# Expert rows that carry their place and weight, in a one-core decoder layer

## The chip, the core and the metric

The kernel runs on one core of a Trainium2 chip. The metric is the device time of one launch in microseconds (us). Five engines work side by side: PE (TensorE) with its weight loads (PEld), DVE (VectorE), ACT (ScalarE), POOL (GpSimd) and SP (SyncE, which here issues plain DMAs). They meet only through semaphores and barriers.

## What is computed

Four sequences of 512 tokens with 256 features go through a Mamba block, a self- and cross-attention block and this feed-forward block; the change lies in the last one:

```python
abel_out = gelu(xn @ abel_w + abel_b)
logits = xn @ moe_gate_w + moe_gate_b
topw, topi = top_k(logits, 2); topw = softmax(topw)
w_dense = sum(one_hot(topi, 8) * topw[..., None], axis=-2)
h = gelu(einsum('bsd,edh->ebsh', xn, ew1) + eb1)
eo = einsum('ebsh,ehd->ebsd', h, ew2) + eb2
moe_out = einsum('ebsd,bse->bsd', eo, w_dense)
for i in range(3): moe_out = moe_out @ expm(gens[i])
gate = sigmoid(concatenate([abel_out, moe_out]) @ gc_w + gc_b)
return residual + abel_out * (1 - gate) + moe_out * gate
```

There are 8 experts with 512 hidden features, and each of the 2048 tokens goes to 2 of them: 4096 rows in all.

## The kernel before

The program is a row of blocks with barriers between them. Block b = 0 to 4 (`for b in range(NB + 1)`) begins sequence b (projections, convolution, time steps) and ends sequence b-1 (output projection, residual, norms, the abel branch, routing). Between them lie the scan and the attention of sequence b, which the change leaves alone. I call blocks 1 to 3 the middle blocks and b = 4, which only ends, the last block.

**Routing** (end of a block, `choose`, `place`, `weigh`). DVE picks two experts a token. TensorE counts how many tokens of each expert stand ahead (`rank_mm`). `place` (L726) turns this into row numbers in `rows_in`, a DRAM tensor with a region of 2048 rows for each expert, and writes them to `route`; `weigh` (L742) then works out the two weights of each token. When the row numbers are there (`route_ready`), POOL scatters the normalised rows `xn2` in 8 indirect DMAs of 128 rows (L503), then adds the abel branch to the residual x1 (L508). SP stores what is kept for later: `kept_sel`, `kept_abel`, `kept_res`, `kept_route` (L465).

**Expert part** (from L1406). 23 tiles of 256 rows, each of one expert: every expert's rows in whole tiles, then spare ones. DVE works out from the counts which expert and which rows a tile has (L1592 to L1620, the tables) and which bias (L1632 to L1638). SP reads both numbers from the table (`value_load`, L1415 and L1422) and issues the tile's rows (L1427, 256 KB) and weights (L1416 and L1418, 512 KB each; three weight buffers). For a tile PE turns the rows (`rows_up`, L1485), multiplies into the hidden layer (`hidden`, 16 matmul instructions), ACT applies gelu (L1569), PE multiplies into the output (`output`, 16 instructions), DVE copies it to `eo` (L1666) and SP stores that to `rows_out` (L1432). DVE's `rows_down` (L1627) takes the turned rows from PSUM with the norm's scale and shift. PE's order is hidden(i+1), rows_up(i+2), output(i). SP's order for tile i is

```python
rows_load(i + 3)
weights(i + 2)      # waits for the output matmuls of tile i - 1
rows_store(i)       # waits for DVE's copy of tile i
```

and every second tile from 4 on SP brings back a sequence's `kept_abel` and `kept_res` (L1451, L1453).

**Last part.** 16 steps q of 128 tokens. POOL gathers the two expert rows of each token from `rows_out` (L1472, 32 indirect DMAs, buffers for 8 steps) at places that DVE works out in `places`. PE makes the bias part (`biased`, the weights of the token on the experts' `eb2`), DVE adds the two rows times their weights (L1675, L1678), PE turns the sum (L1536), ACT copies it (L1582), PE multiplies it by the rotation `Wrot` (`rotated`). DVE takes the gate's product over the row (L1683) and the difference to the abel branch (L1686); per sequence follow the gate (L1691, L1692, ACT L1575) and the result rows (L1701), which SP stores (L1457). All matmuls there and in the expert part are recorded at L165, transpositions at L1485 and L1536.

## Time and profile before

| | us |
|---|---|
| median of 3 runs (2150.28 to 2151.87) | 2150.67 |
| the profiled execution, its own time | 2149.31 |
| its span in the trace | 2147.6 |
| PE busy | 1607.7 (75%) |
| PEld busy | 768.3 (36%) |
| DVE busy | 1416.9 (66%) |
| ACT busy | 827.5 (39%) |
| POOL busy | 640.9 (30%) |
| mean granted clock of TensorE | 0.866 |

"Granted clock" is the share of TensorE's full speed (1.00 is 2.4 GHz, 0.50 is 1.2 GHz). In rows of the timeline the first number is the start, the second how long a group of instructions took from first start to last end; in brackets stands the idle time of the engine ahead of it and what ended that. A row SPq or POOLq is a DMA issue or a wait on that queue. "remote" is a releaser that the profile doesn't know.

### The profile page before, as it was taken

Reading aid. Unit: us, or ns where it says so; the run is one execution under the profiler, and the core shown is the slowest. Engines: PE = TensorE matmul, PEld = TensorE weight load, DVE = VectorE, ACT = ScalarE, POOL = GpSimd, SP = SyncE. Lnnn points to the kernel's source line nnn. Section 1 sums busy time; section 2 is a strip of 40 time slices with the busy share of each in tenths; the row PEclk is TensorE's granted clock in tenths of the full one; section 3 lists DMA queues with packets and bytes.
Section 4 is the critical chain, followed back from the end, with each engine's and each line's share of the span. In section 5 each row is a group of like instructions: output and inputs, shape, how many; then the busy total and the mean of one; then the engine's idle time right before and its main releaser. Section 6 shows DMA issues by size and latency. Waiting matters only on the chain. (4 is left out here: it accounts for less than half of the span.)

```text
span 2147.6 us, 19868 instructions
## 1 busy us (share of the span) xinstructions
PE 1607.7 (75%) x6786; PEld 768.3 (36%) x6786; DVE 1416.9 (66%) x2091; ACT 827.5 (39%) x1552; POOL 640.9 (30%) x396
## 2 busy tenths in 40 slices
PE   4887699774977898739867997646679984488976
PEld 2454223242543222315432332212322222467753
DVE  6996878277987775659968873779687835221225
ACT  4542166543422566244422664433115661111210
POOL 2763311206655021136532112076340112100041
PEclk9899699986997899959987998789879996799975
DMA  5821720021006220030035200210062100466631
GB/s 178 289 70 47 157 38 1 1 79 45 1 0 167 38 38 1 0 123 1 0 95 109 38 2 0 82 37 0 5 156 41 21 1 9 153 200 196 198 98 61
DMA packets 125101, 149.27 MB, mean 70 GB/s; under 512 B 16000, under 2 KB 107784, under 8 KB 122952
## 3 DMA queue, kind: packets, MB, share of 16 engines
q1 hardware_dynamic: 121928, 139.61, 23.9%
q0 software_dynamic: 3072, 8.39, 1.2%
q8 instruction: 54, 0.88, 0.2%
q14 instruction: 47, 0.39, 0.1%
HBM read 96.47 MB, written 51.09 MB: 69 GB/s over the span
## 5 line engine op out<-in xcount | busy, mean ns | idle before, releaser
L165 PE MATMUL PS<-arena 128*32 128x512 f32 (+11 forms) x4126 | 883.4, 454 | 122.2 <-DMA arena<-in_ew 25.4
L165 PEld LDWEIGHTS PS<-arena 128*32 128x32 f32 (+3 forms) x4126 | 367.1, 128 | 615.8 <-ACT arena L1338 276.5
L1338 ACT ACTIVATE arena<-PS 128x512 f32<-128x512 f32 (+3 forms) x768 | 375.4, 541 | 378.3 <-PE PS L165 377.1
L968 POOL TENSOR_TENSOR arena<-arena 128x1024 f32<-128x1024 f32 x128 | 302.1, 2362 | 186.5 <-DVE arena L992 147.0
L1358 DVE TENSOR_REDUCE maxs<-PS 128x1 f32<-128x1024 f32 x256 | 302.3, 1217 | 78.4 <-PE PS L165 78.3
L992 DVE TENSOR_TENSOR_SCAN arena<-PS,arena 128x1024 f32<-128x1024 f32 x128 | 292.1, 2282 | 9.3 <-POOL arena L968 9.3
L948 ACT ACTIVATE PS<-arena,A_neg 128x511 f32<-128x511 f32 x256 | 166.0, 681 | 261.3 <-DVE arena L992 193.1
L165 PE MATMUL PS<-arena,ident 128*128 128x512 f32 (+1 forms) x560 | 259.8, 590 | 5.4 <-DVE arena L1001 5.4
L1191 POOL TENSOR_TENSOR arena<-xn 128x512 f32<-128x512 f32 x16 | 20.3, 1267 | 585.4 <-ACT xn L1326 585.4
L165 PE MATMUL PS<-bc,bc_sel 96*128 96x512 bf16 x128 | 52.3, 408 | 149.2 <-DVE arena L1001 98.1
L1001 DVE TENSOR_TENSOR arena<-arena,PS 128x1024 f32<-128x1024 f32 x128 | 156.3, 1221 | 7.1 <-PE PS L165 3.0
L1385 DVE RECIPROCAL arena<-arena 128x512 f32<-128x512 f32 x16 | 53.6, 3348 | 142.5 <-POOL arena L1191 142.5
L165 PEld LDWEIGHTS PS<-arena,ident 128*128 128x128 f32 x560 | 109.5, 199 | 91.7 <-issue 74.5
L1362 DVE TENSOR_REDUCE maxs<-PS 128x1 f32<-128x512 f32 (+3 forms) x256 | 106.9, 477 | 19.9 <-PE PS L165 18.8
L1569 ACT ACTIVATE arena<-PS,arena 128x256 f32<-128x256 f32 x92 | 38.6, 471 | 196.2 <-PE PS L165 196.2
L1472 POOL DMA_INDIRECT arena<-rows_out,arena x32 | 30.6, 957 | 239.3 <-DMA rows_out<-arena 224.5
L1627 DVE TENSOR_SCALAR arena<-PS,gam,bet 128x256 f32<-128x256 f32 x46 | 22.9, 539 | 108.3 <-PE PS L1485 108.3
L165 PEld LDWEIGHTS PS<-bc,bc_sel 96*128 96x128 bf16 x128 | 12.5, 98 | 202.6 <-DVE arena L1001 147.2
L503 POOL DMA_INDIRECT rows_in<-arena,route x32 | 34.8, 1089 | 162.4 <-DVE route L739 153.9
L1125 DVE TENSOR_TENSOR arena<-arena 128x512 f32<-128x512 f32 x40 | 50.0, 1249 | 32.9 <-ACT arena L1080 32.9
L1096 POOL TENSOR_TENSOR arena<-arena 128x512 bf16<-128x512 f32 x40 | 46.3, 1157 | 66.9 <-DVE arena L1126 66.9
L165 PE MATMUL PS<-wp,arena 128*128 128x256 f32 x128 | 37.2, 462 | 34.3 <-PEq L172 34.3
(251 smaller groups left out, 1807.8 us busy)
## 6 DMA issues: line engine op xcount, KB each, us to landing
arena<-in_ew SPq DMA_DIRECT2D x46, 512.0 KB, 5.2
arena<-stack_parts SPq DMA_DIRECT2D x288, 64.0 KB, 3.7
rows_in<-nil SPq DMA_DIRECT2D x17, 1024.0 KB, 11.2
arena<-b_rows SPq DMA_DIRECT2D x16, 1024.0 KB, 7.7
stack_parts<-arena SPq DMA_DIRECT2D x40, 384.0 KB, 3.1
arena<-stack_parts SPq DMA_DIRECT2D x96, 128.0 KB, 4.6
arena<-rows_in SPq DMA_DIRECT2D x23, 256.0 KB, 2.9
rows_out<-arena SPq DMA_DIRECT2D x23, 256.0 KB, 2.1
```

Source lines behind the costliest of these rows:

```text
L165: return nc.tensor.matmul(o, l, r, start=start, stop=stop)
L948: last = nc.scalar.activation(decay(i)[:, k, 1:T], delta[:, 2 * kh + k, 1:T], ACT.Exp, scale=A_neg[:, 2 * kh + k, n:n + 1])
L968: nc.gpsimd.tensor_tensor(b_sb[i % 2], u[:, 2 * kh:2 * kh + 2, :], Brow[:, n, :].unsqueeze(1).to_broadcast([P, 2, T]), ALU.mult).then_inc( ...
L992: nc.vector.tensor_tensor_scan(h_sb[i % 2].rearrange(flat), decay(i).rearrange(flat), b_sb[i % 2].rearrange(flat), 0.0, ALU.mult, ALU.add)\
L1001: nc.vector.tensor_tensor(g_sb[i % 2], h_sb[i % 2], bank(6).unsqueeze(1).to_broadcast([P, 2, T]), ALU.mult).then_inc(S["g_done"], 1)
L1096: nc.gpsimd.tensor_tensor(pt[i % NPT][:, 2, :], r_sb[i % 2], pt[i % NPT][:, 1, :], ALU.subtract)\
L1125: link(nc.vector.tensor_tensor(r_sb[i % 2], f_sb[i % 2], pt[i % NPT][:, 0, :], ALU.subtract))
L1338: nc.scalar.activation(probs[(HG * s + h) % NPR][:, 0:N], bank(4 + n % 2)[:, 0:N], ACT.Exp, scale=HD ** -0.5).then_inc(S["ring_read"], 1)
L1358: last = nc.vector.reduce_max(maxs[:, g % 2, r, h:h + 1], PS[:, 2 * s:2 * s + 2, :].rearrange("p a n -> p (a n)"), AXX)
L1362: last = nc.vector.reduce_max(maxs[:, g % 2, q, HG + h:HG + h + 1], bank(2 * s + c_)[:, 0:(q + 1) * P], AXX)
L1385: nc.vector.reciprocal(R2, R1).then_inc(S["norm_ready"], 1)
L1569: nc.scalar.activation(hid[i % 2][:, m, :], o, ACT.Gelu, bias=eb1_of[:, i, m:m + 1])\
```

## The change

A row in `rows_in` grows from 256 to 272 numbers: the 256 features, at 256 the number of the place where its result belongs (first or second choice, times 2048, plus the token), at 257 the token's weight, then zeros. For this POOL writes places and a second copy of the rows into `xn2`, and DVE's `weigh` now runs ahead of `place`, since the weight goes out with the row. Rows that no token fills carry the place 4096, which the scatter leaves out.

Of the 23 tiles the first eight are fixed: tile e is the first 256 rows of expert e. The tables are only worked out for the other 15. The weights of the first three tiles are loaded in the last block, into memory that it doesn't use.

In the expert part DVE copies each row's place and weight out of the loaded rows (`noted`), scales the output by the weight as it takes it from PSUM, and POOL scatters it straight to its place in `picked_rows` (two indirect DMAs a tile, 46 in all). SP no longer stores results, and asks for weights i+3 as soon as the output matmuls of tile i are done; the kept tensors come behind them, one every second tile.

In the last part SP reads plain pieces of `picked_rows`. DVE adds the two rows with one operation. The bias part is multiplied through the rotation once, ahead of the tiles (`eb2R`), and joins the rotation's accumulation; the gate's product is a 257th column of the rotation (`turn`), so DVE's product over the row is gone, and `kept_route` with it.

```diff
-NTILE = (TOPK * NB * T + NE * (RT - 1)) // RT
-SPARE = NTILE - TOPK * NB * T // RT
-ROWS = NE * CAP + SPARE * RT
+NEXTRA = (TOPK * NB * T - 1) // RT
+NTILE = NE + NEXTRA
+ROWS = NE * CAP + RT
+RW = 272
+AT_ID, AT_W = DM, DM + 1
+NOWHERE = TOPK * NB * T
...
-    rows_in = nc.dram_tensor("rows_in", (ROWS, DM), F32).ap()
-    rows_out = nc.dram_tensor("rows_out", (NTILE * RT, DM), F32).ap()
+    rows_in = nc.dram_tensor("rows_in", (ROWS, RW), F32).ap()
+    picked_rows = nc.dram_tensor("picked_rows", (NOWHERE, DM), F32).ap()
...
+                    if not begins:
+                        for i in range(NWB):
+                            weights_load(sp, i, i)
...
-                        sp.wait_ge(S["route_ready"], TT + 2)
-                        keep(kept_route[b - 1], route[:].rearrange("p f t -> p (f t)"))
                         if not begins:
-                            sp.wait_ge(S["kept"], 4 * 16)
+                            sp.wait_ge(S["kept"], 3 * 16)
...
+                        nc.gpsimd.memset(xn2[:, :, :, AT_W + 1:RW], 0.0).then_inc(S["rows_told"], 1)
+                        for j in range(TOPK):
+                            nc.gpsimd.iota(xn2[:, j, :, AT_ID], pattern=[[P, TT]], base=(j * NB + b - 1) * T,
+                                           channel_multiplier=1, allow_small_or_imprecise_dtypes=True)\
+                                .then_inc(S["rows_told"], 1)
+                        nc.gpsimd.tensor_copy(xn2[:, 1, :, 0:DM], xn2[:, 0, :, 0:DM]).then_inc(S["rows_told"], 1)
+                        pool.wait_ge(S["rows_told"], 4)
+                        pool.wait_ge(S["weighed"], 2)
                         pool.wait_ge(S["route_ready"], 1)
                         for t in range(TT):
                             for j in range(TOPK):
                                 nc.gpsimd.indirect_dma_start(
                                     rows_in, bass.IndirectOffsetOnAxis(ap=route[:, j, t:t + 1].bitcast(I32), axis=0),
-                                    xn2[:, t, :], None).then_inc(rows_stored, 16)
+                                    xn2[:, j, t, :], None).then_inc(rows_stored, 16)
...
                 def weights(i):
-                    if i >= NWB:
-                        sp.wait_ge(S["eo_mm"], i - NWB + 1)
-                    e = sp.value_load(where[0:1, 0, i:i + 1].bitcast(I32), min_val=0, max_val=NE - 1)
-                    sp.dma_start(ew1[i % NWB], w["ew1"][bass.ds(e, 1), :, :].rearrange("a (k p) n -> p (a k) n", p=P))\
-                        .then_inc(weights_in[i % NWB], 16)
-                    sp.dma_start(ew2[i % NWB], w["ew2"][bass.ds(e, 1), :, :].rearrange("a (k p) n -> p (a k) n", p=P))\
-                        .then_inc(weights_in[i % NWB], 16)
-
+                    sp.wait_ge(S["eo_mm"], i - NWB + 1)
+                    if i < NE:
+                        e = i
+                    else:
+                        if i == NE:
+                            sp.wait_ge(S["tables"], 1)
+                        e = sp.value_load(where[0:1, 0, i - NE:i - NE + 1].bitcast(I32), min_val=0, max_val=NE - 1)
+                    weights_load(sp, i, e)
 
                 def rows_load(i):
                     if i >= NXB:
-                        sp.wait_ge(S["rows_mm"], i - NXB + 1)
-                    sp.dma_start(rows[i % NXB], rows_in[bass.ds(row(i), RT), :].rearrange("(r p) n -> p r n", p=P))\
+                        sp.wait_ge(S["rowsT_ready"], KM * (i - NXB + 1))
+                    if i < NE:
+                        r = i * CAP
+                    else:
+                        if i == NE:
+                            sp.wait_ge(S["tables"], 1)
+                        r = sp.value_load(where[0:1, 1, i - NE:i - NE + 1].bitcast(I32), min_val=0, max_val=ROWS - RT)
+                    sp.dma_start(rows[i % NXB], rows_in[bass.ds(r, RT), :].rearrange("(r p) n -> p r n", p=P))\
                         .then_inc(rows_back[i % NXB], 16)
 
-                def rows_store(i):
-                    sp.wait_ge(S["eo_ready"], i + 1)
-                    sp.dma_start(rows_out[i * RT:(i + 1) * RT, :].rearrange("(r p) n -> p r n", p=P), eo[i % 3])\
-                        .then_inc(eo_stored[i % 3], 16)
-
-                sp.wait_ge(S["tables"], 1)
-                rows_load(0)
-                weights(0)
-                rows_load(1)
-                weights(1)
-                rows_load(2)
-                back(route_all.rearrange("p b f t -> p b (f t)"), kept_route.rearrange("b p f -> p b f"))
-                back(sel_all.rearrange("e (b t) -> e b t", b=NB), kept_sel.rearrange("b e t -> e b t"))
+                def pick(q):
+                    if q >= NPK:
+                        sp.wait_ge(S["summed"], q - NPK + 1)
+                    src = picked_rows.rearrange("(j q p) n -> q p j n", j=TOPK, p=P)
+                    sp.dma_start(picked[q % NPK], src[q]).then_inc(picked_in[q % NPK], 16)
+
+                sp.wait_ge(rows_stored, 16 * TOPK * TT * NB)
+                for i in range(3):
+                    rows_load(i)
+                sp.dma_start(sel_all.rearrange("e (b t) -> e b t", b=NB), kept_sel.rearrange("b e t -> e b t"))\
+                    .then_inc(S["sel_back"], 16)
                 for i in range(NTILE):
                     if i + 3 < NTILE:
                         rows_load(i + 3)
-                    if i + 2 < NTILE:
-                        weights(i + 2)
-                    rows_store(i)
-                    if i >= 4 and i % 2 == 0 and i < 4 + 2 * NB:
-                        b = i // 2 - 2
-                        sp.dma_start(ab_all[:, TT * b:TT * (b + 1), :], kept_abel[b].rearrange("(t p) n -> p t n", p=P))\
-                            .then_inc(S["rest_back"], 16)
-                        sp.dma_start(res_all[:, TT * b:TT * (b + 1), :], kept_res[b].rearrange("(t p) n -> p t n", p=P))\
-                            .then_inc(S["rest_back"], 16)
+                        weights(i + 3)
+                    if i % 2 == 0 and i < 4 * NB:
+                        b, part = i // 4, i % 4
+                        if part == 0:
+                            sp.dma_start(ab_all[:, TT * b:TT * (b + 1), 0:DM],
+                                         kept_abel[b].rearrange("(t p) n -> p t n", p=P)).then_inc(S["rest_back"], 16)
+                        else:
+                            sp.dma_start(res_all[:, TT * b:TT * (b + 1), :],
+                                         kept_res[b].rearrange("(t p) n -> p t n", p=P)).then_inc(S["rest_back"], 16)
+                for i in range(NEB):
+                    sp.wait_ge(eo_stored[i], 16 * RS * len(range(i, NTILE, NEB)))
+                for q in range(NQ):
+                    pick(q)
...
-                pool.wait_ge(S["moved"], 1)
-                for i in range(3):
-                    pool.wait_ge(eo_stored[i], 16 * len(range(i, NTILE, 3)))
-                for q in range(NQ):
-                    if q >= NGB:
-                        pool.wait_ge(S["summed"], q - NGB + 1)
-                    for j in range(TOPK):
+                for i in range(NTILE):
+                    pool.wait_ge(S["noted"], 2 * (i + 1))
+                    pool.wait_ge(S["eo_ready"], RS * (i + 1))
+                    for r in range(RS):
                         nc.gpsimd.indirect_dma_start(
-                            picked[j][q % NGB], None, rows_out,
-                            bass.IndirectOffsetOnAxis(ap=slot[:, q // TT, j, q % TT:q % TT + 1].bitcast(I32),
-                                                      axis=0)).then_inc(picked_in[q % NGB], 16)
+                            picked_rows,
+                            bass.IndirectOffsetOnAxis(ap=row_id[i % NIB][:, r:r + 1].bitcast(I32), axis=0),
...
                     last.then_inc(S["moeT_mm"], 1)
 
                 def rotated(q):
-                    pe.wait_ge(S["moeT_ready"], q + 1)
                     if q >= 4:
                         pe.wait_ge(S["diffed"], q - 3)
+                    o = bank(4 + q % 4)[:, 0:DM + 1]
+                    mm(o, sel_all[:, q * P:(q + 1) * P], eb2R, True, False)
+                    pe.wait_ge(S["moeT_ready"], q + 1)
                     for k in range(KM):
-                        last = mm(bank(4 + q % 4)[:, 0:DM], moeT[q % 2][:, k, :], Wrot[:, k, :], k == 0, k == KM - 1)
+                        last = mm(o, moeT[q % 2][:, k, :], turn[:, k, :], False, k == KM - 1)
                     last.then_inc(S["rot_mm"], 1)
 
...
+                    nc.vector.tensor_copy(row_id[i % NIB].bitcast(I32), rows[i % NXB][:, :, AT_ID]).then_inc(S["noted"], 1)
+                    nc.vector.tensor_copy(row_w[i % NIB], rows[i % NXB][:, :, AT_W]).then_inc(S["noted"], 1)
...
+                dve.wait_ge(rows_stored, 16 * TOPK * TT * NB)
+                nc.vector.tensor_copy(turn[:, :, 0:DM], Wrot[:]).then_inc(S["turn_ready"], 1)
+                for k in range(KM):
+                    nc.vector.tensor_tensor_reduce(out=dots2, in0=Wrot[:, k, :], in1=gcw[:, DM:2 * DM], scale=1.0,
+                                                   scalar=0.0, op0=ALU.mult, op1=ALU.add,
+                                                   accum_out=turn[:, k, DM:DM + 1]).then_inc(S["turn_ready"], 1)
+                    dve.wait_ge(S["turn_ready"], 2 + k)
                 rows_down(0)
+                extra_tiles()
                 rows_down(1)
...
+                    dve.wait_ge(S["noted"], 2 * (i + 1))
+                    if i >= NEB:
+                        dve.wait_ge(eo_stored[i % NEB], 16 * RS * (i // NEB))
+                    for r in range(RS):
+                        nc.vector.tensor_scalar(eo[i % NEB][:, r, :], bank(6 + i % 2)[:, r * DM:(r + 1) * DM],
+                                                row_w[i % NIB][:, r:r + 1], None, ALU.mult).then_inc(S["eo_ready"], 1)
 
                 def summed(q):
-                    dve.wait_ge(picked_in[q % NGB], 32 * (q // NGB + 1))
-                    dve.wait_ge(S["eb_mm"], q + 1)
+                    dve.wait_ge(picked_in[q % NPK], 16 * (q // NPK + 1))
                     if q >= NAB:
                         dve.wait_ge(S["moeT_mm"], q - NAB + 1)
-                    b, t = q // TT, q % TT
-                    link(nc.vector.scalar_tensor_tensor(acc[q % NAB], picked[0][q % NGB],
-                                                        route_all[:, b, TOPK, t:t + 1],
-                                                        bank(q % 2)[:, 0:DM], ALU.mult, ALU.add))
-                    nc.vector.scalar_tensor_tensor(acc[q % NAB], picked[1][q % NGB], route_all[:, b, TOPK + 1, t:t + 1],
-                                                   acc[q % NAB], ALU.mult, ALU.add).then_inc(S["summed"], 1)
-
-                def gated(q):
+                    nc.vector.tensor_tensor(acc[q % NAB], picked[q % NPK][:, 0, :], picked[q % NPK][:, 1, :], ALU.add)\
+                        .then_inc(S["summed"], 1)
+
+                def differ(q):
                     dve.wait_ge(S["rot_mm"], q + 1)
-                    link(nc.vector.tensor_tensor_reduce(out=dots2, in0=bank(4 + q % 4)[:, 0:DM],
-                                                        in1=gcw[:, DM:2 * DM], scale=1.0, scalar=0.0,
-                                                        op0=ALU.mult, op1=ALU.add, accum_out=gates[:, 0, q:q + 1]))
-                    nc.vector.tensor_tensor(ab_all[:, q, :], bank(4 + q % 4)[:, 0:DM], ab_all[:, q, :], ALU.subtract)\
-                        .then_inc(S["diffed"], 1)
+                    nc.vector.tensor_tensor(ab_all[:, q, :], bank(4 + q % 4)[:, 0:DM + 1], ab_all[:, q, :],
+                                            ALU.subtract).then_inc(S["diffed"], 1)
 
```

SP in the expert part, between the weights of one tile and those of the next. Before:

```order
L1415 TENSOR_LOAD arena [waits eo_mm]
L1415 ISA x2
L1416 ISA
L1416 DMA arena<-in_ew 128x2x512
L1418 DMA arena<-in_ew 128x4x256
L1432 DMA rows_out<-arena 128x2x256 [waits eo_ready]
L1422 TENSOR_LOAD arena [waits rows_mm]
L1422 ISA x2
L1427 ISA
L1427 DMA arena<-rows_in 128x2x256
```

With the change:

```order
L1432 TENSOR_LOAD arena [waits eo_mm]
L1432 ISA x2
L465 ISA
L465 DMA arena<-in_ew 128x2x512
L467 DMA arena<-in_ew 128x4x256
L1443 TENSOR_LOAD arena [waits rowsT_ready]
L1443 ISA x2
L1444 ISA
L1444 DMA arena<-rows_in 128x2x272
```

The store, and with it the wait for DVE's copy (`eo_ready`), is gone from SP's queue, and the rows wait for DVE's `rows_down` instead of for PE.

DVE at the end of a middle block, around the row numbers. Before (`fchain` is the chain of these small operations):

```order
L734 TENSOR_TENSOR s_pos<-PS,base 128x32 [waits rank_mm,fchain]
L737 TENSOR_TENSOR s_nth<-s_gt,s_pos 128x32 [waits fchain]
L738 TENSOR_REDUCE row_f<-s_nth 128x4 [waits fchain]
L737 TENSOR_TENSOR s_nth<-s_eq,s_pos 128x32 [waits fchain]
L738 TENSOR_REDUCE row_f<-s_nth 128x4 [waits fchain]
L739 CAST route<-row_f 128x8 [waits fchain]
L740 TENSOR_TENSOR base<-base,PS 128x8
L744 TENSOR_SCALAR s_den<-sel_e 128x4 [waits sel_e,fchain]
```

With the change:

```order
L754 TENSOR_SCALAR s_den<-sel_e 128x4 [waits sel_e,fchain]
L755 RECIPROCAL s_den<-s_den 128x4 [waits fchain]
L756 TENSOR_TENSOR sel<-sel,sel_ex 128x32 [waits fchain]
L757 TENSOR_TENSOR sel<-sel,s_den 128x32 [waits fchain]
L760 TENSOR_TENSOR s_nth<-s_gt,sel 128x32 [waits sel_ready]
L761 TENSOR_REDUCE arena<-s_nth 128x4 [waits fchain]
L760 TENSOR_TENSOR s_nth<-s_eq,sel 128x32 [waits weighed]
L761 TENSOR_REDUCE arena<-s_nth 128x4 [waits fchain]
L767 TENSOR_TENSOR s_pos<-PS,base 128x32 [waits rank_mm,weighed]
```

Eight operations of the weighing stand ahead of the placing now; the CAST to `route`, for which POOL waits, comes after them.

PE in the last part, one step. Before:

```order
L1536 MATMUL PS<-ident,arena 128x128 [waits moeT_ready,summed]
L1536 MATMUL PS<-ident,arena 128x128
L165 MATMUL PS<-eb,arena 128x256 [waits summed]
L165 MATMUL PS<-Wrot,arena 128x256 [waits diffed,moeT_ready]
L165 MATMUL PS<-Wrot,arena 128x256
```

With the change:

```order
L1555 MATMUL PS<-ident,arena 128x128 [waits moeT_ready,summed]
L1555 MATMUL PS<-ident,arena 128x128
L168 MATMUL PS<-arena 128x257 [waits diffed]
L168 MATMUL PS<-arena 128x257 [waits moeT_ready]
L168 MATMUL PS<-arena 128x257
```

The number of matmuls stays, with one column more each; the bias matmul is now the first of the rotation's accumulation.

## Rows read from the trace of the kernel before

**Rows 1.** stretches: us, busy (instructions) of PE, PEld, DVE, ACT, POOL, PEclk, DMA, GB/s
```profile
1853.80:2060.00 206.20, 179.94 (x821) 152.10 (x820) 42.66 (x93) 40.12 (x94) 0.00 (x0) 0.96 0.59 184
2060.00:2147.60 87.60, 55.43 (x128) 32.54 (x128) 37.09 (x113) 6.63 (x20) 30.62 (x32) 0.53 0.25 75
```

**Rows 2.** chain of waits, expert part: start us, us, what
```profile
1866.57 0.70 DVE arena L1666
...
1868.87 0.28 SPq L1415
...
1870.07 5.14 DMA arena<-in_ew
1875.25 3.72 PE PS L165 x16
1878.97 0.44 PE PS L1485 x4
1879.41 3.47 PE PS L165 x16
...
1967.08 6.90 DMA arena<-in_ew
...
2045.47 13.83 PE PS L165 x64
2059.32 0.70 DVE arena L1666
```

**Rows 3.** waits of SP's queue, expert part to the end: us, times, longest
```profile
SPq L1432 <- DVE arena L1666: 133.1, 23, 12.7
```

**Rows 4.** timeline, end of the first middle block: start us, us, what
```profile
491.78 0.17 DVE L744 TENSOR_SCALAR s_den<-sel_e 128x4 f32<-128x4 f32 x1
...
493.32 0.19 DVE L751 TENSOR_REDUCE route<-s_nth 128x4 f32<-128x32 f32 x1
...
506.18 0.50 SPq L465 DMA_DIRECT2D kept_route<-route  x1
```

**Rows 5.** timeline, convolution in the first middle block, beside POOL
```profile
445.39 2.58 POOL L498 TENSOR_TENSOR x<-x,arena 128x1024 f32<-128x1024 f32 x1 [16.49 <-DVE arena L663]
...
445.80 4.29 DVE L690 SCALAR_TENSOR_TENSOR arena<-arena,conv_w 128x512 f32<-128x512 f32 x3
...
450.59 2.33 DVE L690 SCALAR_TENSOR_TENSOR arena<-arena,conv_w 128x512 f32<-128x512 f32 x3
```

**Rows 6.** timeline, from the barrier to the first tile
```profile
1838.47 0.07 DVE L1592 MEMSET arena<- 128x8 f32 x1 [13.46 <-PEq L461]
...
1844.42 0.41 SPq L1427 DMA_DIRECT2D arena<-rows_in  x1
...
1847.14 0.72 PEld L1485 LDWEIGHTS PS<-ident,arena 128*128 128x128 f32 x4 [25.09 <-DMA arena<-rows_in]
...
1853.76 1.06 PE L165 MATMUL PS<-arena 128*128 128x256 f32 x2
```

**Rows 7.** timeline, last part, DVE, PE and ACT
```profile
2068.32 0.69 PE L1536 MATMUL PS<-ident,arena 128*128 128x128 f32 x2 [7.13 <-DVE arena L1678]
...
2088.14 0.39 ACT L1582 ACTIVATE arena<-PS 128x256 f32<-128x256 f32 x1 [9.07 <-remote]
...
2104.95 0.82 ACT L1582 ACTIVATE arena<-PS 128x256 f32<-128x256 f32 x2 [16.42 <-remote]
...
2115.12 0.63 PE L1536 MATMUL PS<-ident,arena 128*128 128x128 f32 x2
...
2118.70 0.63 PE L1536 MATMUL PS<-ident,arena 128*128 128x128 f32 x2
...
2142.57 1.67 DVE L1701 SCALAR_TENSOR_TENSOR arena<-arena 128x256 f32<-128x256 f32 x4
```

**Rows 8.** two short stretches of the last part, columns as in rows 1
```profile
2115.00:2120.00 5.00, 5.00 (x13) 2.86 (x11) 2.98 (x10) 0.77 (x2) 0.00 (x0) 0.50 0.00 0
2076.00:2080.00 4.00, 4.00 (x10) 2.40 (x10) 2.42 (x9) 0.38 (x1) 3.08 (x4) 0.50 0.37 106
```

279 lines of the change are left out of this document (133 added, 146 removed).

## The prediction

> **What bounds the kernel now.** I read the busy time by stretches first, then the chain of waits, then the timeline at the joints. The expert part takes 206.2 us and the last part 87.6 us [rows 1]; the rest of the span, 1853.8 us, is the attention and scan part, which the change touches only at four places. In the expert part TensorE is busy 179.9 of 206.2 us at a mean granted clock of 0.96, the DMA engines 0.59: neither is full. The chain shows why. One turn covers two tiles: the result copy on DVE (1866.57), SP's store and address work, a flight of the next weights (5.14), then 3.72 + 0.44 + 3.47 of matmuls to the next copy [rows 2]. The weights of tile i+3 can be asked for only when SP has come past the store of tile i, and SP sat 133.1 us in those 23 waits [rows 3]. So the turn is weight latency plus one tile of TensorE work, and not two tiles of work.
>
> The last part is TensorE at half clock: the granted clock is 0.53 [rows 1], one step of 16 starts every 3.58 us (2115.12 to 2118.70) [rows 7], and inside 2115 to 2120 TensorE is busy 5.00 of 5.00 us at 0.50 [rows 8]. There are holes on top: ACT sat idle 9.07 and 16.42 us before two copies whose inputs had long been made [rows 7], released by nothing the profile can name. They lie where POOL issues one gather after another, 3.08 us of 4 [rows 8].
>
> **The sum, part by part** (against the profiled span, 2147.6 us).
>
> 1. *Three middle blocks.* The weighing now stands ahead of the placing, so the row numbers come later by what those eight DVE operations take: 491.78 to 493.51, 1.73 us [rows 4]. POOL's eight scatters wait for these numbers, and the barrier waits for what follows them. The store of the routing table, 0.50 us on SP ahead of the barrier [rows 4], goes. POOL also gets a small memset, two iotas and a copy of 1024 elements a partition. They end long before POOL needs the routing, but beside a POOL operation of that size DVE's three convolution steps took 4.29 us where they take 2.33 [rows 5], and the copy falls on the same steps. The copy's own time is not in the trace: bounds are 0 (it misses them) and 1.96 us (the whole difference); I take 1.2, nearer the row, as the copy reads one input and that addition two. Per block +1.73 - 0.50 + 1.2 = 2.4, three times +7.3 us. The Trainium skill (SBUF — State Buffer, "Who interferes with whom") says that a DVE instruction with two SBUF inputs waits out a GpSimd instruction that reads SBUF, whole. By that rule each block would pay up to the copy's full length. The 4.29 us agree with it.
>
> 2. *Into the first tile.* The last such block pays 1.73 us and about 0.5 of the copy (its DVE work there reads PSUM), so the barrier moves from 1838.47 to 1840.7 [rows 6]. Behind it stood the tables and the first weights: rows issued at 1844.42, their transposes at 1847.14, the first expert matmul at 1853.76 [rows 6]. Now the first eight tiles have fixed places, three tiles of weights are loaded during the last block, and the rows go out at once: issue 0.41 and flight 2.3 (1844.83 to 1847.14) give 1843.4. TensorE first makes the turned bias: about 1.7 us of DVE work, then four instructions at 0.53 (two took 1.06 [rows 6]), to 1844.5; transposes and the copies down about 2.4 more. First matmul at 1846.9: -6.8 us. Bounds: -9 without the bias work in the way, -4 if the copies go slowly.
>
> 3. *First tiles.* Tile 1's rows now come up behind the first hidden layer, so its hidden layer waits for a copy down: a transposition and two copies at low clock, 2.5 us. The new tables (some 25 small DVE operations) lie beside the first hidden layer. +2.5 us.
>
> 4. *Steady tiles.* SP no longer stores; it waits for the output matmuls of tile i and asks for weights i+3 at once. From the read of the expert's number to the landing a turn takes 6.34 us (1868.87 to 1875.21) [rows 2]; add 0.9 for scatters in the same queue engines (a gather pair moves 106 GB/s at a share of 0.37 [rows 8], so 256 KB are about 0.9 us of all engines). 7.2 us stand against 3.46 + 0.44 + 3.47 = 7.4 us of TensorE work on tiles that are already there (64 matmuls took 13.83, so 16 take 3.46 [rows 2]). The weights just fit. From the first result (1866.57) to the last output matmul (2059.32) were 192.8 us [rows 2]. The work in it is 43 groups of 16 and 20 transpositions: 43 x 3.46 + 20 x 0.44 = 157.6. As the fit is tight I add 8 us of small waits (0.4 a tile; bounds 0 and 20, the latter if each second tile waits 2 us). -27.2 us. DVE has two copies and two scaled results a tile and POOL two scatters: both under half of 7.4 us, with three result buffers. The kept tensors are now behind the weights in SP's queue, where today they are ahead of them: the flight of 6.90 us [rows 2] should go.
>
> 5. *Joint.* Today from the last output matmul to the first transposition of the last part 9.0 us pass (2059.32 to 2068.32) [rows 2, 7]: copy, store, gather. Now: two scaled copies, two scatters, their landing, a plain read. About 9.6, +0.6 us.
>
> 6. *Last part.* Plain reads replace 32 gathers; the gate's product rides as column 257 of the rotation; the bias matmul moves into the rotation's accumulation. TensorE keeps its instructions: 16 x 3.58 = 57.3 us if the clock stays. After the last rotation DVE has one difference, a clamp, ACT's exponential, two small operations and 1.67 us of results [rows 7]: about 3.3 us, 60.6 in all. Today 75.9 (2068.32 to 2144.24) [rows 7]. -15.3 us: some 13 from the holes, which end with the burst of gathers, 2 from shorter DVE work behind the last rotation.
>
> Sum: +7.3 - 6.8 + 2.5 - 27.2 + 0.6 - 15.3 = -38.9 us, a span of 2108.7. The profiled execution took 2149.31 us, 1.7 more than its span, and the median of the runs is 1.4 above it: 2108.7 + 3.1 = **2112 us**.
>
> **Rivals.**
>
> *The clock rises in the last part* (0.20). For: without the bias matmul in between, today's last steps run on at 2136 us and the clock comes up right behind them; the continuous expert part is at 0.96 [rows 1]. Against: 5.00 of 5.00 busy at 0.50 [rows 8], for over 20 us, with the same instructions that the change keeps. At 2.4 GHz a step is six instructions at 0.216, transpositions and the same gaps, about 2.1 us; 16 x 1.5 = 23 us less: 2089. The Trainium skill (TensorE: Matmul & The Clock Gate, "Part 1: The HAM clock gate") says that the throttled state is the default and activity releases it. By that rule the time is 2089; the 0.50 at full busy time speaks against it here.
>
> *The holes come with indirect DMAs wherever they are* (0.10). The last part lost 13 us over 32; 46 are now spread over the expert part. For: nothing in the trace names their cause. Against: the 32 scatters of the blocks show none. +13 us: 2125.
>
> *Weights still pace the tiles* (0.08). With the scatters in the way the flight becomes 6.90 + 0.9, the latency 9.0, and a tile costs (9.0 + 7.36)/2 = 8.2 instead of 7.16 + 0.36. 22 x 0.68 = +15: 2127.
>
> *Slower than before* (0.03). The same loop, with scattered rows of 1 KB and weights fighting for the DMA engines: each weight load then lands late and TensorE idles, falling to half clock between tiles. The whole gain is gone when the stretch of point 4 costs 38.9 us more than forecast, (165.6 + 38.9)/22 = 9.3 us a tile, so a latency of 11.2 us, a flight near 10 where 5.14 and at most 6.90 are seen [rows 2]. At a flight of 11 the time is 2112 + 38.9 + 11 = 2162.
>
> **How the numbers follow.** The forecast has 0.59, with its own range 2102 to 2123 from the bounds of points 1, 2 and 4. The range 2086 to 2128 takes in the clock case and the two cases above 2120. A measurement of this kernel tells 0.2% (4 us) from no change. Faster by more: all but the last rival and its edge, 0.95; within 0.02; slower 0.03.
>
> **What would show it.** Right: SP waits for TensorE's output matmuls, not for DVE's copy; a tile starts each 7.2 to 7.8 us; the first expert matmul stands some 7 us nearer to the barrier and more; steps of 3.6 us in the last part with no unnamed idle time; blocks one to three 2 to 3 us longer each. Wrong: TensorE waiting for weights in most tiles, a granted clock of 1.0 in the last part, or unnamed idle time in the expert part.

## The result

| | before | changed |
|---|---|---|
| median of 4 runs each | 2150.53 us | 2097.24 us |
| lowest to highest | 2150.28 to 2151.87 | 2095.23 to 2100.65 |
| span of the profiled execution | 2147.6 us | 2093.5 us |

The ratio is 0.9753, with a 95% interval from 0.9736 to 0.977: 53 us less, where 38.9 were forecast. The time lies in the range given, 15 us below the forecast. The kernel before is not always at 2150: beside four of the experiments (weights asked for first, the margin, the first idle gathers, the filling matmuls), which ran on another chip than the later ones, it took 2133 us, beside all others 2149 to 2151. I call these four the first group. The changed kernel itself was not timed beside the 2133; with added work that nothing waits for it took 2097.93 us there. The experiments show where most of these 17 us lie.

Busy time by stretches of the changed kernel: from the first expert matmul to the last result, and the last part. The columns are those of [rows 1].

```profile
1848.78:2020.10 171.32, 169.26 (x824) 148.15 (x824) 52.95 (x180) 40.13 (x94) 42.92 (x44) 1.00 0.64 203
...
2028.69:2086.90 58.21, 58.17 (x128) 33.38 (x128) 17.79 (x52) 6.43 (x19) 0.00 (x0) 0.50 0.27 88
```

In the expert part TensorE went from 179.9 of 206.2 us [rows 1] to 169.3 of 171.3, at full clock throughout. In the last part it is busy 58.17 of 58.21 us at 0.50.

The chain of waits through the steady tiles, which answers to [rows 2] (start us, us, what):

```profile
1854.88 3.69 PE PS L168 x16
1858.57 0.44 PE PS L1503 x4
1859.01 6.91 PE PS L168 x32
1865.92 0.44 PE PS L1503 x4
1866.35 6.91 PE PS L168 x32
```

There is no transfer and no copy on it any more: a tile costs 7.35 us (6.91 + 0.44), and this goes on to 2020.02. SP's waits in the whole kernel at the two lines that ask for weights (L1432 is the address read in `weights`, L465 the load itself), and TensorE's from 1850 to 2020 (engine, line, waited for: us in total, times, longest):

```profile
SPq L1432 <- PE PS L168: 63.3, 15, 4.6
SPq L465 <- PE PS L168: 34.0, 4, 16.9
```

```profile
PE PS L168 <- DVE arena L1624: 2.0, 1, 2.0
```

SP now waits for TensorE and not for DVE's copy [rows 3]. TensorE's only wait there is the 2.0 us before its second hidden layer.

The timeline at the four places of the other changes:

```profile
457.51 2.98 DVE L711 SCALAR_TENSOR_TENSOR arena<-arena,conv_w 128x512 f32<-128x512 f32 x3
...
457.73 1.43 POOL L518 COPY arena<-arena 128x1024 f32<-128x1024 f32 x1
...
493.98 0.17 DVE L772 CAST route<-row_f 128x8 int32<-128x8 f32 x1
...
505.20 2.35 POOL L529 TENSOR_TENSOR x<-x,arena 128x1024 f32<-128x1024 f32 x1
...
508.56 4.65 POOL L984 TENSOR_TENSOR arena<-arena 128x1024 f32<-128x1024 f32 x2 [1.02 <-POOLq L473]
...
1843.08 1.40 SPq L1444 DMA_DIRECT2D arena<-rows_in  x3
...
1846.28 1.12 PE L1503 MATMUL PS<-ident,arena 128*128 128x128 f32 x4
...
1848.78 3.69 PE L168 MATMUL PS<-arena 128*128 128x256 f32 x16 [1.39 <-DVE arena L1624]
...
1862.50 0.88 DVE L1683 TENSOR_SCALAR arena<-PS,arena 128x256 f32<-128x256 f32 x2 [2.32 <-PE PS L168]
...
2020.05 0.87 DVE L1683 TENSOR_SCALAR arena<-PS,arena 128x256 f32<-128x256 f32 x2 [2.58 <-PE PS L168]
...
2028.69 1.28 PE L1555 MATMUL PS<-ident,arena 128*128 128x128 f32 x4 [8.68 <-DVE arena L1690]
...
2032.92 0.63 PE L1555 MATMUL PS<-ident,arena 128*128 128x128 f32 x2
...
2036.51 0.63 PE L1555 MATMUL PS<-ident,arena 128*128 128x128 f32 x2
...
2088.22 1.68 DVE L1709 SCALAR_TENSOR_TENSOR arena<-arena 128x256 f32<-128x256 f32 x4
```

Read against the same points of before ([rows 2], [rows 6], [rows 7]), the 54.1 us between the spans divide as follows. The third column is the prediction's term, cut at the same points (the 2.2 us of point 2 for the barrier stand in the first row).

| stretch | measured | forecast |
|---|---|---|
| to the barrier: 1838.47 to 1843.07 | +4.6 | +9.5 |
| barrier to first expert matmul: 15.3 to 5.7 | -9.6 | -9.1 |
| first expert matmul to first result: 12.8 to 13.7 | +0.9 | +2.5 |
| first to last result: 192.8 to 157.6 | -35.2 | -27.2 |
| last result to first step of the last part: 9.0 to 8.6 | -0.4 | +0.6 |
| first step to the last output on DVE: 75.9 to 61.2 | -14.7 | -15.3 |
| behind it: 3.4 to 3.6 | +0.2 | 0 |

The row of the first result depends on the clock: in this execution it was at 1.00 from the first hidden layer on. In a second execution of the changed kernel (under "The holes of the last part") the same stretch took 16.0 us and not 13.7, since the clock was still at the lower level when the first hidden layer began (columns as above):

```profile
1851.10:1855.00 3.90, 3.84 (x9) 3.15 (x10) 3.27 (x18) 0.05 (x1) 0.00 (x0) 0.50 0.04 10
```

### The profile page after: what moved, and what is told of

Its sections match the earlier page's. It is cut to its first block and busy times, and to the rows that moved or that the text cites. A ratio compares the mean times of both kernels' runs of the same rounds, so it can differ in the third digit from the quotient of the medians.

```text
span 2093.5 us, 19873 instructions
## 1 busy us (share of the span) xinstructions
PE 1611.3 (77%) x6792; PEld 767.3 (37%) x6792; DVE 1406.0 (67%) x2088; ACT 828.1 (40%) x1554; POOL 660.2 (32%) x427
## 5 line engine op out<-in xcount | busy, mean ns | idle before, releaser
L168 PE MATMUL PS<-arena 128*128 128x256 f32 (+9 forms) x4226 | 929.0, 458 | 97.2 <-ACT arena L1354 23.4
L168 PEld LDWEIGHTS PS<-arena 128*32 128x32 f32 (+4 forms) x4226 | 389.9, 131 | 607.5 <-ACT arena L1354 276.9
L1489 POOL DMA_INDIRECT picked_rows<-arena x46 | 45.4, 986 | 135.4 <-DVE arena L1683 114.8
L168 PE MATMUL PS<-xT,in_w 128*128 128x512 f32 x128 | 58.5, 616 | 3.4 <-DVE xT L813 3.4
L1595 ACT ACTIVATE arena<-PS,arena 128x256 f32<-128x256 f32 x60 | 25.2, 471 | 85.2 <-PE PS L168 85.2
```

The lines of the kernel that those rows point to most:

```text
L168: return nc.tensor.matmul(o, l, r, start=start, stop=stop)
L1489: nc.gpsimd.indirect_dma_start(picked_rows, bass.IndirectOffsetOnAxis(ap=row_id[i % NIB][:, r:r + 1].bitcast(I32), axis=0), eo[i % NEB][:, ...
```

## The experiments

The ratio given with each run is that of its median to that of the kernel before, measured beside it on the same chip, with its 95% interval. The texts in quotes are the expectations, as they stood before each run.

### Weights asked for first

In the kernel before, in SP's queue:

```diff
                 weights(1)
                 rows_load(2)
+                weights(2)
...
-                    if i + 2 < NTILE:
-                        weights(i + 2)
+                        weights(i + 3)
                     rows_store(i)
```

> The kernel before, with one edit in the expert part's SP queue: the weights of tile i+3 are asked for as soon as the output matmuls of tile i are done, ahead of the store of tile i; nothing else. Theory (the order of the queue is the whole gain of the steady tiles): from the end of the output matmuls to the landing about 0.5 + 0.5 + 5.1 = 6.1 to 6.7 us, against 7.36 us of TensorE work that is there; the waits go, the stretch from the first result to the last output matmul falls from 192.8 to 158 to 162 us, the time to 2116 to 2122 us. Rival (the stores and their traffic matter too): every second tile still waits 1 to 2 us, the stretch stays above 172 us, the time above 2130.

Measured: 2104.17 us, ratio 0.9857 [0.9841, 0.9873]; the kernel before took 2133.13 beside it. The waits of TensorE in the expert part, of the kernel before:

```profile
PE PS L165 <- DMA arena<-in_ew: 25.4, 13, 5.7
```

and of this one:

```profile
PE PS L165 <- DMA arena<-in_ew: 0.7, 1, 0.7
```

From the first to the last result 161.0 us pass (1870.74 to 2031.69) where it was 192.8. So 31.8 of the 35.2 us come from one thing, when SP asks; a second execution on another chip gave 160.8. The time came out lower than both theories said because the last part, with its 32 gathers in place, took 61.0 us and had no unnamed idle time at all. This is as long as the last part of the changed kernel (61.2). The new one saves some 3 us of DVE work behind the last rotation, but the old one has two shorter steps at its end (2.13 us from 2091.07 to 2093.20), which make no bias matmul and in which the clock rises. The missing holes spoke against the cause that the prediction names for the holes and led to the next three groups.

### The margin of the fit

In the changed kernel, on SP:

```diff
                     sp.wait_ge(S["eo_mm"], i - NWB + 1)
+                    sp.wait_ge(S["eo_ready"], RS * (i - NWB + 1))
```

> The changed kernel; SP asks for the weights of tile i+3 only when DVE has also scaled and copied the result of tile i (about 0.9 us later). Measures the margin of the fit. Theory (the flight is still near 5.1 us beside the scatters, so some 1.0 us of margin): 0 to +3 us on 2097. Rival (the fit is bare, the flight longer beside scatters): each steady tile waits 0.5 to 0.9 us, +10 to +18 us.

Measured: 2105.3 us, ratio 0.9867 [0.9848, 0.9885]. First to last result takes 164.9 us, 7.4 more, of which the waits show 4.6:

```profile
PE PS L168 <- DMA arena<-in_ew: 4.6, 8, 2.3
```

The other 2.6 us stand in TensorE's own busy time (160.11 us against 157.51). The time lies between what both theories give (8 us more than 2097): a delay of 0.9 us makes TensorE wait for weights eight times. The margin is real but under a microsecond for a third of the tiles. "The weights just fit" was right; the allowance of 8 us for it was too large. It was not for nothing, either: of eight executions in which this stretch of the changed kernel was left as it is, three took 157.6 to 157.7 us, four 158.2 to 159.6 and one 161.0, that one with three waits for weights, 2.7 us together.

### The holes of the last part

First with gathers added to the changed kernel, whose data nobody reads; POOL issues them behind its last scatters:

```diff
+                for q in range(NQ):
+                    g, had = ghost_in[q % 4]
+                    if q >= 4:
+                        pool.wait_ge(g, had + 32 * (q // 4))
+                    if q >= 8:
+                        pool.wait_ge(S["summed"], q - 7)
+                    for j in range(TOPK):
+                        nc.gpsimd.indirect_dma_start(
+                            ghost[2 * (q % 8) + j], None, rows_in,
+                            bass.IndirectOffsetOnAxis(ap=route[:, j, q % TT:q % TT + 1].bitcast(I32),
+                                                      axis=0)).then_inc(g, 16)
```

> The changed kernel; beside its last part POOL issues the 32 indirect gathers that the kernel before had there, one row of 1088 bytes a partition, into buffers that nobody reads; nothing waits for them. Theory (the unnamed holes of the part come with the burst of indirect DMAs): ACT and DVE stand still again for some 10 to 16 us, the last part takes 71 to 77 instead of 61 us, the time 2107 to 2113. Rival (the holes were the gathers' own late data, which the profile failed to name): 0 to +3 us.

Measured: 2097.93 us, no unnamed idle time. This looked like a refutation, but the kernel before took 2133.13 beside it, 17 less than at first. So both kernels ran again, unchanged:

> The kernel before, unchanged. In the run with the weights asked for first, the burst of 32 gathers was there and ran without one unnamed idle time, last part 61.0 us; with 32 idle gathers added to the changed kernel likewise. Theory (the holes of the profiled run are no property of the kernel but of that run): the last part takes about 63 us from the first transposition to the last output instead of 75.9, no idle time without a name, span 2131 to 2136. Rival (they belong to this kernel's own burst, which starts at another moment than in the other two): the holes are there again at the same steps, span near 2147.

> The changed kernel, unchanged, beside the others of this call. Both theories: 2095 to 2099, no unnamed idle time; it gives the ratio against the kernel before in the same hour, 0.982 to 0.984 if the holes were of that run alone, 0.975 if not.

Measured: the kernel before 2150.74 (the other runs of it beside the experiments of this group 2149.22), the changed one 2098.61, ratio 0.9763 [0.9744, 0.9783]. The holes of the kernel before are back at the same steps, of the same length as in [rows 7]:

```profile
2089.05 0.38 ACT L1582 ACTIVATE arena<-PS 128x256 f32<-128x256 f32 x1 [10.06 <-remote]
...
2105.16 0.82 ACT L1582 ACTIVATE arena<-PS 128x256 f32<-128x256 f32 x2 [15.74 <-remote]
```

The theory as it was written fell: the holes are no accident of one execution. What was left was a condition that holds for a whole group of runs and only shows with some kernels. Two kernels of the first group were run again, on a third chip, to tell whether it is the gathers:

> The kernel before with the weights asked for first, a second time, since the kernel before ran in 2133 us beside its first run and in 2149 beside the later ones. Theory (the holes are a state of the hour, whatever the kernel that has the gathers): if the kernel before takes 2149 in this call too, the holes are in this run's last part as well, 74 to 76 us instead of 61.0, the time 2117 to 2120. Rival (they depend on where the burst falls): no holes, 2104, whatever the kernel before takes. If the kernel before takes 2133 in this call, it tells nothing new on this.

> The changed kernel with 32 idle gathers beside its last part, a second time, for the same reason. Theory (in the hours in which the kernel before takes 2149, a burst of indirect gathers brings the holes): 10 to 16 us of unnamed idle time, 2107 to 2113. Rival (the holes need gathers whose data DVE waits for, or this burst is not enough): 2098.

Measured, with the kernel before at 2149.28: weights first 2115.93 us, ratio 0.9841 [0.9826, 0.9857], 12 more than in the first group, its last part 75.6 us in place of 61.0. Idle gathers 2118.55 us, ratio 0.9854 [0.9839, 0.9869], 20 more than the changed kernel. The timeline of the latter:

```profile
2029.65 0.99 POOL L1507 DMA_INDIRECT arena<-rows_in,route  x1 [1.92 <-issue]
...
2047.43 0.38 ACT L1624 ACTIVATE arena<-PS 128x256 f32<-128x256 f32 x1 [6.30 <-remote]
...
2059.36 0.43 DVE L1712 TENSOR_TENSOR arena<-PS,arena 128x257 f32<-128x257 f32 x1 [14.04 <-remote]
...
2064.95 0.38 ACT L1624 ACTIVATE arena<-PS 128x256 f32<-128x256 f32 x1 [17.14 <-remote]
...
2068.62 0.95 POOL L1507 DMA_INDIRECT arena<-rows_in,route  x1 [0.30 <-issue]
...
2074.78 0.42 DVE L1712 TENSOR_TENSOR arena<-PS,arena 128x257 f32<-128x257 f32 x1 [14.39 <-remote]
```

ACT and DVE are idle for up to 17 us although their inputs are there for most of that time (ACT's copy at 2064.95 had its two transpositions at 2050.84); POOL issues one gather each 1.25 us all the while, and some 5 us behind its last one the stand-still ends. Nothing waits for these gathers, so it is not their data. Last, the same 32 gathers, each pair behind the sum of its step:

```diff
-                    if q >= 8:
-                        pool.wait_ge(S["summed"], q - 7)
+                    pool.wait_ge(S["summed"], q + 1)
```

> The changed kernel with the same 32 idle gathers beside its last part, now one pair to a step of TensorE (each pair waits for the sum of its step, so POOL issues for 2.5 of each 3.6 us and not without a break). In the run before, the first stand-still came 14.6 us after the first of the unbroken burst (17.8 us in the kernel before) and the last ended with it. Theory (it is the unbroken burst): no unnamed idle time, 2097 to 2100. Rival (the number or the mean rate of the gathers is what counts): holes from some 15 us in, 2108 or more. If the kernel before takes 2133 in this call, it tells nothing.

Measured: 2099.7 us, ratio 0.9768 [0.9751, 0.9784], the kernel before at 2151.13. No idle time without a name is left. The gathers did not come in pairs, though, as the expectation has it. DVE's sums run ahead of the steps, so POOL found most pairs released already: 16 in a row (19.8 us), a pause of 7.0 us, eight, a pause of 4.5 us, eight:

```profile
2029.29 0.99 POOL L1506 DMA_INDIRECT arena<-rows_in,route  x1 [5.31 <-DVE arena L1706]
...
2048.11 0.95 POOL L1506 DMA_INDIRECT arena<-rows_in,route  x1 [0.30 <-issue]
2056.08 0.94 POOL L1506 DMA_INDIRECT arena<-rows_in,route  x1 [7.02 <-DVE arena L1706]
...
2070.57 0.94 POOL L1506 DMA_INDIRECT arena<-rows_in,route  x1 [4.54 <-DVE arena L1706]
...
2079.32 0.95 POOL L1506 DMA_INDIRECT arena<-rows_in,route  x1 [0.30 <-issue]
```

So the gathers bring the holes, but not their data and not their number alone: two pauses took all of them away. With 30 or 32 in a row the first stand-still began 15 to 19 us behind the first gather, after 12 to 16 of them; the longest row here is 16. That fits a limit on the unbroken run. Whether it is that or the mean rate over the whole (32 in 51 us in place of 40) no run tells apart. The bursts of eight in the blocks (10.1 us) and the 46 scatters of the expert part, two a tile, show none. Open too is what the engines wait for, and why 32 in a row cost nothing in the first group: it ran at another time and on another chip than the later groups, and the two can't be told apart.

### The clock of the last part

In the changed kernel, on TensorE, ahead of the last part, 20 matmuls whose result nobody reads:

```diff
+                for _ in range(20):
+                    mm(bank(0)[:, 0:RT], rowsT[0][:, 0, 0:P], rowsT[1][:, 0, :], True, True)
                 pe.wait_ge(S["eo_ready"], RS * NTILE)
```

> The changed kernel; TensorE makes 20 matmuls of 128x256 (40 instructions, 8.6 us at full clock) into an unused bank between the last output matmul and the first transposition of the last part. Theory (the pause of 8.6 us is what lets the clock fall, and the last part would hold it): the granted clock is 1.0 in the last part, a step 1.8 us in place of 3.60, the last part 33 instead of 61 us, the time near 2069. Rival A (the last part's steps cannot hold the clock): it starts at 1.0 and falls back within it, gain in between, 2075 to 2092. Rival B (no effect): 2097.

Measured: 2087.55 us, ratio 0.9786 [0.9769, 0.9804] with the kernel before at 2133.13, some 10 less than the changed kernel. Rival A holds: the last part starts at 1.00 with steps of 1.91 us and falls back after 25 us. The timeline shows the waits, the busy time by stretches the clock:

```profile
2047.82 0.44 PE L1555 MATMUL PS<-ident,arena 128*128 128x128 f32 x2 [1.34 <-DVE arena L1692]
...
2057.02 0.44 PE L1555 MATMUL PS<-ident,arena 128*128 128x128 f32 x2 [1.34 <-DVE arena L1692]
2057.39 3.11 PE L168 MATMUL PS<-arena 8*128 8x257 f32 x6
```

```profile
2050.00:2055.00 5.00, 5.00 (x22) 3.23 (x21) 1.74 (x7) 1.24 (x4) 0.00 (x0) 1.00 0.00 0
2055.00:2060.00 5.00, 3.66 (x12) 2.13 (x11) 3.29 (x9) 0.38 (x1) 0.00 (x0) 0.75 0.30 105
```

Each fourth step TensorE waited 1.34 us for DVE, which had four results of a block in a row ahead of the next sum. Behind the second such wait (the third of any length; one of 0.17 us stands at the start) the clock fell, and the same steps then took 3.6 us, without any wait, to the end. The next kernel takes these waits away, and the wait before the second hidden layer as well:

```diff
                 rows_up(0)
+                rows_up(1)
                 hidden(0)
-                rows_up(1)
...
                 rows_down(0)
+                rows_down(1)
                 extra_tiles()
-                rows_down(1)
...
-                    if q % TT == 3 and q > TT:
-                        mixed(q // TT - 1)
+                    if q >= TT + 3:
+                        mixed((q - TT - 3) // TT, range((q + 1) % TT, (q + 1) % TT + 1))
...
```

The 20 filling matmuls are in it too; `mixed` now takes the steps it has to do.

> The changed kernel with the 20 filling matmuls in the joint; DVE's results of a block spread one to a step instead of four in a row (the four made TensorE wait 1.34 us at every fourth step, and behind the third such wait the clock fell); and at the start the rows of tile 1 are turned ahead of the first hidden layer, the tables of the extra tiles made behind them. Theory: steps of 1.91 us without those waits, the granted clock 1.0 to the end, the last part 16 x 1.91 + 4 = 34.6 us against 61.2; the second hidden layer starts behind the first one without the idle 1.97 us, about 1.4 us earlier; in all 2097 - 26.6 - 1.4 = 2069, range 2066 to 2074. Rival (the steps at full clock do not hold it, the waits were only its occasion): it falls after some 25 us in the last part as before, 2084 to 2088.

Measured: 2068.39 us (2067.54 to 2073.72), ratio 0.9627 [0.9613, 0.9641]: 81 us less than before and some 30 less than the changed kernel. From first step to last output 35.2 us (2031.52 to 2066.68), at full clock; TensorE's last matmul ends some 3.3 us ahead of that, and up to there it has next to no idle time:

```profile
2031.50:2066.70 35.20, 31.43 (x129) 19.70 (x128) 20.12 (x59) 6.62 (x20) 0.00 (x0) 1.00 0.44 146
```

That the two waits made the clock fall rests on this pair of kernels, one profiled execution each, on two chips.

In the first tiles the second hidden layer now follows on the first (32 instructions in one piece, 1852.61 to 1860.80). The first result stands 12.3 us behind the first expert matmul, although the clock was low at its start in this execution; the changed kernel took 13.7 us with the clock at 1.00 and 16.0 with it low:

```profile
1851.49 1.11 PE PS L1503 x4
1852.61 8.19 PE PS L168 x32
1860.80 0.44 PE PS L1503 x4
```

### The two costs in the blocks

In the kernel before, the eight weighing operations are moved out of `weigh` to stand in `place` ahead of its wait, and POOL's wait for the row numbers counts them too; the first lines of them:

```diff
+                        dve.wait_ge(S["sel_e"], 2)
+                        fed(nc.vector.tensor_scalar(s_den[:], sel_e2[:], 1.0, None, ALU.add))
...
                         dve.wait_ge(S["rank_mm"], 1)
```

> The kernel before, with the eight weighing operations of DVE put ahead of the placing ones; nothing else. Theory (the scatters' instructions on POOL are longer beside those DVE operations, 1.48 to 1.77 us where 0.97 is usual): the row numbers come 1.75 us later, the eight scatters take 10.1 instead of 10.8 us from the first to the addition behind them, so each block and the barrier behind the last pay 1.0 us, 4 us in all. Rival (the scatters' lengths have another cause): 1.75 us each, 7 us in all.

Measured: 2155.01 us, ratio 1.0026 [1.0015, 1.0037]. From the first addition of the first middle block on POOL to the next block's start 62.96 us pass, against 61.72 and 62.02 in two executions of the kernel before; over all three middle blocks it is 1.1 us a block more than the mean of the old code. The scatters are shorter as expected. The second one, before and here:

```profile
494.11 1.48 POOL L503 DMA_INDIRECT rows_in<-arena,route  x1 [0.31 <-issue]
```

```profile
494.95 0.98 POOL L503 DMA_INDIRECT rows_in<-arena,route  x1 [0.31 <-issue]
```

The eight took 10.2 us in place of 10.8. Three blocks at 1.1 us and 0.6 in the last are 3.8 of the 4 us expected. The ratio alone would not decide: its interval is 3 to 8 us and takes in the rival's 7.

In the changed kernel, the copy goes from POOL to ACT, behind its gelu:

```diff
-                        nc.gpsimd.tensor_copy(xn2[:, 1, :, 0:DM], xn2[:, 0, :, 0:DM]).then_inc(S["rows_told"], 1)
+                        act.wait_ge(S["fxn_ready"], 2 * TT)
+                        nc.scalar.activation(xn2[:, 1, :, 0:DM], xn2[:, 0, :, 0:DM], ACT.Copy)\
+                            .then_inc(S["rows_told"], 1)
```

> The changed kernel, with the copy of the 1024 elements a partition (the second set of rows) made by ACT behind its gelu and not by POOL. Theory (POOL's copy holds DVE up): the three convolution steps take 2.3 again instead of 2.98 us, each middle block is 0.65 us shorter, 2 us in all, 2095 against 2097. Rival (the copy costs nothing on the path, or ACT's copy holds DVE up as well): within 0.5 us of the unchanged kernel in the same stretch.

Measured: 2100.1 us, ratio 0.9763 [0.9743, 0.9783], not to be told from the changed kernel's 2098.61. The convolution steps are back at 2.33 us:

```profile
457.70 2.33 DVE L713 SCALAR_TENSOR_TENSOR arena<-arena,conv_w 128x512 f32<-128x512 f32 x3
```

But the first middle block shortened by 0.25 to 0.35 us only (62.75 against 63.00 and 63.09), the second by 0.3 to 0.4, and the third by 1.5 to 1.9, for which nothing here gives a reason. POOL's copy does hold DVE up, by 0.65 us on these three; about half of that arrives at the end of the first two blocks. The whole is too small for the times to settle.

## Why the prediction was right, and where it was off

**The mechanism of point 4 was right, its allowance was not.** Asking earlier takes the weights off the path; the first experiment shows it alone. The 157.6 us of work counted from [rows 2] are the measured stretch to 0.1 us. The 8 us added for small waits measured nothing in this execution, and at most 3.4 us in the seven others with the same expert part. This is the largest part of the error, 8.0 of 15.2 us. A value near the bound of 0 was the one to take, as nothing in the rows called for 0.4 us a tile. The rival that the weights still pace the tiles did not come, though 0.9 us of delay would have begun it.

**Point 1** was put at 2.4 us a block. It measured 1.4, 1.05 and 1.2 in the two executions compared (61.72 to 63.09, 61.91 to 62.96, 61.93 to 63.10), and 1.0 in the mean of 12 old and 24 new blocks (61.94 to 62.97). The 1.73 us of weighing are there, but three terms were off. The copy was taken at 1.2 us and held DVE up by 0.65, of which some 0.3 arrived. The store that goes was put at 0.50 us; the wait behind POOL's addition shrank by 0.35 (1.37 to 1.02 us). And a gain was missed: the scatters had been beside those eight operations, and without them the eight take 0.7 us less. Together 1.73 + 0.3 - 0.35 - 0.7 = 1.0. The rule that was weighed there, of the Trainium skill (SBUF — State Buffer, "Who interferes with whom"), would have allowed up to the copy's whole length, which is 1.43 us. One of the three steps took 1.41 us where the others took 0.75; as the first had begun 0.22 us ahead of the copy, less than the whole copy was left to wait out, and the trace does not speak against the rule. In the last such block +2.2 were forecast for the barrier; from its first addition to the barrier it took 0.5 more (39.17 to 39.66). Together +4.6 stand against +9.5. Executions of the same code differ by up to 5 us at this point (1837.8 to 1842.9 in four of the old code, 1842.9 to 1846.8 in nine of the new); the mean difference is 5 us.

**Points 2, 3 and 5** were each right to 0.5 to 1.6 us. Into the first tile 5.7 us behind the barrier, 6.2 forecast. TensorE's wait at the second hidden layer is the one that point 3 names; behind the tables of the extra tiles it was 2.0 us. The term came out at 0.9 and not 2.5 because the clock was at 1.00 from the first hidden layer on. That was luck of the execution: in the second one it came out at 3.2.

**Point 6** was right in size, -14.7 against -15.3, and its split into 13 us of holes and 2 of shorter DVE work was not. The steps kept 3.60 us at half clock (3.58 forecast), and the holes went with the burst of gathers. But the old last part without holes takes 61.0 us and the new one 61.2, so the holes are the whole gain: the shorter DVE work is there, some 3 us, and is lost again because now the last two steps take 3.6 us like all others. The idle gathers show that it is the burst and not the waiting for data. What the prediction could not see is that these holes, 14.6 us of the last part (75.6 against 61.0), are not always there. Without them, in the first group, the changed kernel with its idle gathers is 35 us faster than the kernel before (2133.13 to 2097.93, ratio 0.983), not 53, and the kernel before with nothing but the weights asked for first has 29 of these 35 (2104.17). The kernel before was not profiled in that group; the holes account for most of its 17 us, and the rest is not shown. The rival that holes come with indirect DMAs wherever they are had the right culprit and the wrong condition: 46 of them in the expert part, two at a time, cost nothing.

**The clock** stayed at its lower level, as said. The rule of the Trainium skill (TensorE: Matmul & The Clock Gate, "Part 1: The HAM clock gate"), that activity releases the throttle, would have given 2089; 58.17 busy of 58.21 us at 0.50 speak against it here. Coming from the other side the same steps ran at 1.00 to their end, 32 us with TensorE busy 31.43 us. In these runs the steps kept the level at which they began, until two waits of 1.34 us in one of them. Why busy steps at half clock do not bring it up is open. One rival is untested: the clock did rise in places where TensorE had larger matmuls only. It went from 0.50 (1851 to 1855) to 1.00 (from 1860 on) in the first tiles of the second execution of the changed kernel, and in the kernel before it rose in the last two steps, which no longer have the small bias matmul of 8 rows (0.84 over 2136 to 2140). In the changed kernel every step has that matmul, to the end.

## What to carry to other kernels

Where a ring of buffers is refilled from a queue, look at what stands ahead of the request in that queue: a store that waits for a copy cost 32 us here, and moving the request in front of it needed no other change. Give a long run of indirect DMAs pauses, or put plain transfers in its place: 32 in a row cost 12 to 20 us on all occasions but one, the same 32 with two pauses of 4.5 and 7.0 us nothing. And time the kernel before again beside every experiment, as it moved by 17 us between groups of runs. Before a stage of small matmuls, keep TensorE going through the pause in front of it and take the waits out of its first steps: 20 matmuls of no use and a reordered DVE queue brought that stage from 61.2 to 35.2 us.

## What was not expected of the hardware

- ACT and DVE stood still up to 17.9 us with their inputs ready while POOL issued 30 or 32 indirect DMAs without a break; the first stand-still began 15 to 19 us after the first DMA, the last ended some 5 us behind the end of the unbroken run. In the first group of runs, on another chip than the later ones, such bursts cost nothing.
- The granted clock stayed at 0.50 for 58 us with TensorE busy without a gap, and at 1.00 for 32 us in the same steps when it had been 1.00 before them. In the run with the filling matmuls alone it fell behind two waits of 1.34 us, four steps apart.
- POOL's second indirect scatter of a block took 1.48 us in the first middle block and 1.76 in the others beside small DVE operations, and 0.98 and 1.04 without them.
